# Second attention of a two-layer kernel: the output's division moves from VectorE to GpSimd, and its four turnings are spread over the loop

## What is computed

```
x = ln(x + block0(x))            # causal attention, 16 heads of 8, and more
x = ln(x + x @ w.T + pooled(x) @ disha)
qkv = x @ Wqkv + bqkv            # the second attention: no mask
scores = q @ k.T / sqrt(8)       # 16 heads, 1024 x 1024 per batch and head
attn = softmax(scores)
out = attn @ v                   # (sum of exp * v) / (sum of exp)
x = ln(x + out @ Wout + bout)
x = ln(x + relu(x @ W1 + b1) @ W2 + b2)
```

## Time and profile before

| | |
|---|---|
| median of 3 runs | 1514.3 us (1511.41 to 1517.33) |
| the profiled execution, its own time | 1513.78 us |
| its span in the trace | 1512.0 us |
| granted PE clock, mean over the span | 0.964 |
| PE busy over the span | 1366.1 us (90%) |
| DVE busy | 1251.6 us (83%) |
| ACT busy | 1079.6 us (71%) |
| POOL busy | 278.4 us (18%) |

### The profile page before, as it was taken

One profiled execution on the slowest core, in us unless ns is written; L12 is line 12 of the kernel. 1 busy time (PEld: TensorE's weight loads), 2 busy tenths in 40 slices (PEclk: granted clock), 3 DMA queues, 4 the chain that ended last, 5 costly groups with the idle time before them and its releaser, 6 DMA issues.

```text
span 1512.0 us, 31977 instructions
## 1 busy us (share of the span) xinstructions
PE 1366.1 (90%) x13016; PEld 565.2 (37%) x13016; DVE 1251.6 (83%) x1715; ACT 1079.6 (71%) x1239; POOL 278.4 (18%) x624
## 2 busy tenths in 40 slices
PE   6699999999998768888679999999999999999886
PEld 3334434444443235456323332332333333323455
DVE  8988888888884386985899999999999999997043
ACT  6167777777777567763358888888888888888652
POOL 5022313222222151431100000000000000001252
PEclk9689999999999989999889999999999999999998
DMA  5510111101000000021110000000000000000001
GB/s 179 169 44 24 39 31 31 40 24 46 24 4 2 1 1 0 1 81 67 42 64 24 23 24 23 24 21 14 16 23 24 23 23 24 3 3 3 1 15 42
DMA packets 38995, 47.90 MB, mean 32 GB/s; under 512 B 11072, under 2 KB 20160, under 8 KB 38720
## 3 DMA queue, kind: packets, MB, share of 16 engines
q1 hardware_dynamic: 38416, 45.31, 9.8%
q10 hardware_dynamic: 432, 0.53, 0.1%
HBM read 30.22 MB, written 15.47 MB: 30 GB/s over the span
## 4 chain that ended last, share of the span: by engine, by line
PE 73%; DVE 11%; ACT 7%; issue 5%; POOL 3%; DMA 1%; ACTq 0%; POOLq 0%; SPq 0%; DVEq 0%
PE ps L428 29%; PE ps L406 15%; PE ps L385 12%; PE ps L554 7%; DVE l_negp L326 3%; PE ps L445 3%; ACT l_outT L304 2%; ACT shared L298 2%; POOL n_rs L516 2%; PE ps L391 2%; DVE n_bst L497 1%; PE ps L547 1%; PE ps L1042 1%; PE ps L910 1%; PE ps L562 1%
## 5 line engine op out<-in xcount | busy, mean ns | idle before, releaser
L326 DVE TENSOR_REDUCE l_negp<-ps 128x2 f32<-128x1024 f32 (+2 forms) x832 | 956.4, 1181 | 57.7 <-PE ps L391 33.3
L298 ACT ACTIVATE shared<-ps 128x1024 f32<-128x1024 f32 (+1 forms) x832 | 820.5, 991 | 185.3 <-PE ps L406 155.7
L428 PE MATMUL ps<-shared,l_vs 128*32 128x256 f32 (+3 forms) x6648 | 515.4, 385 | 18.9 <-ACT l_outT L304 14.1
L385 PE MATMUL ps<-Ks,Qs 48*128 48x512 bf16 (+3 forms) x1792 | 329.2, 368 | 31.1 <-DVE l_negp L326 22.0
L406 PE MATMUL ps<-Qs,Ks 51*128 51x512 bf16 (+3 forms) x1792 | 321.1, 367 | 14.5 <-ACT shared L298 6.3
L428 PEld LDWEIGHTS ps<-shared,l_vs 128*32 128x32 f32 x6648 | 136.6, 108 | 198.0 <-issue 163.4
L406 PEld LDWEIGHTS ps<-Qs,Ks 51*128 51x128 bf16 x1792 | 81.1, 93 | 316.8 <-issue 181.3
L385 PEld LDWEIGHTS ps<-Ks,Qs 48*128 48x128 bf16 x1792 | 87.5, 94 | 171.8 <-ACT shared L298 96.0
L282 POOL TENSOR_SCALAR_AFFINE_SELECT shared<-shared 128x512 f32<-128x512 f32 x128 | 81.7, 640 | 311.1 <-ACT shared L298 309.0
L267 POOL CAST l_parts<-l_negm 128x16 bf16<-128x16 f32 x64 | 12.6, 197 | 442.3 <-DVE l_negm L331 439.2
L391 PE MATMUL ps<-mask,id 64*128 64x128 bf16 x1024 | 68.5, 222 | 0.0
(11 more groups left out here) (160 smaller groups left out, 1094.7 us busy)
## 6 DMA issues: line engine op xcount, KB each, us to landing
Qs<-scr_q SPq DMA_DIRECT2D x128, 64.0 KB
Ks<-scr_k SPq DMA_DIRECT2D x64, 96.0 KB
Qs<-scr_q SPq DMA_DIRECT2D x128, 32.0 KB
Ks<-scr_k SPq DMA_DIRECT2D x64, 64.0 KB
scr_q<-own SPq DMA_DIRECT2D x4, 768.0 KB, 3.6
scr_q<-shared SPq DMA_DIRECT2D x4, 768.0 KB, 3.5
scr_k<-own SPq DMA_DIRECT2D x4, 768.0 KB, 4.9
scr_k<-shared SPq DMA_DIRECT2D x4, 768.0 KB, 4.8
```

The costliest lines, as they stand in the source:

```text
L298: act.activation(dst, src, ACT.Exp, scale=SCALE).then_inc(exped, 1)
L326: dve.tensor_reduce(dst, src, AX_X, ALU.max, negate=True).then_inc(reduced, 1)
L385: last = pe.matmul(outs[par], Qs[s][r:r + MROW, h2, qt * P:(qt + 1) * P], Ks[s][r:r + MROW, h2, at:at + w], start=True, stop=True)
L428: last = pe.matmul(pv_ps[32 * h:32 * h + 32, a:a + wide], vs[g % 2][:, kt, h, :], pT[m % PRING][:, h, a:a + wide], start=m == u.first_step ...
```

## The change

For q = 32 to 61 the division leaves DVE. ACT copies what the turnings left in RING, 144 columns (4 query tiles x 4 heads x 8 values and their sum), to `sums` in SBUF, at tick E + 8; POOL raises the sums to the power -1 (a tensor of -1.0 as exponent) and multiplies into `attn_tm`. `sums` has two buffers; the copy waits for the division of two half groups back. RING is free for the next "turn_max" when ACT has copied. For q = 32 to 62 the four turnings stand at E + 4, E + 5, E + 7 and E + 8, each behind that tick's weigh step; q = 63 and the first attention keep all four at E + 4, and q = 62 and 63 keep the division on DVE. The pieces of the diff are, in this order, of `Units.order`, `gpsimd`, `scalar`, `vector`, `slot_free` and `tensor`.

```diff
+def turn_at(q):
+    return (4, 5, 7, 8) if NPER <= q < 2 * NPER - 1 else (4, 4, 4, 4)
+def off_vector(q):
+    return NPER <= q < 2 * NPER - QH
...
-                    (self.k_ends[q] + 2, ("evacuate", q)), (self.k_ends[q] + 4, ("turn_out", q))]
+                    (self.k_ends[q] + 2, ("evacuate", q)), (self.k_ends[q] + turn_at(q)[-1], ("turn_out", q))]
+            out += [(self.k_ends[q] + at, ("turn_part", q, t)) for t, at in enumerate(turn_at(q)[:-1])]
...
+        elif entry[0] == "turn_out" and off_vector(entry[1]):
+            q = entry[1]
...
+            pool.wait_ge(out_copied, q - NPER + 1)
+            pool.wait_ge(normed, q)
+            pool.tensor_tensor(rc[:, :, :], sums[q % 2][:, :, :, HD], minus_one[:, :, :], ALU.pow).then_inc(recips, 1)
+            pool.wait_ge(recips, q + 1)
...
+            pool.tensor_tensor(dst.rearrange("p t (h d) -> p t h d", d=HD), sums[q % 2][:, :, :, 0:HD],
+                               rc[:, :, :].unsqueeze(3).to_broadcast([P, CT, GH, HD]), ALU.mult).then_inc(normed, 1)
...
+        elif entry[0] == "turn_out" and off_vector(entry[1]):
+            q = entry[1]
+            act.wait_ge(out_turned, q + 1)
+            if q >= NPER + 2:
+                act.wait_ge(normed, q - 1)
...
+            act.activation(sums[q % 2][:, :, :, :], src[:, :, :, 0:HD + 1], ACT.Copy).then_inc(out_copied, 1)
...
-        elif entry[0] == "turn_out":
+        elif entry[0] == "turn_out" and not off_vector(entry[1]):
...
+        elif kind == "turn_out" and not off_vector(i):
+            pe.wait_ge(normed, i + 1)
         elif kind == "turn_out":
-            pe.wait_ge(normed, i + 1)
+            pe.wait_ge(out_copied, i - NPER + 1)
...
-            for t in range(CT):
-                last = pe.transpose(to[:, t * P:(t + 1) * P], outT[:, t * P:(t + 1) * P], ident)
-            last.then_inc(out_turned, 1)
+            last = pe.transpose(to[:, t * P:(t + 1) * P], outT[:, t * P:(t + 1) * P], ident)
+            if t == CT - 1:
+                last.then_inc(out_turned, 1)
```

More of the change, by code:

```diff
@@ L166, in order @@
             out += [(self.m_ends[q] - ahead, ("split", q)), (self.m_ends[q] - 1 - ahead + 4, ("turn_max", q)),
-                    (self.k_ends[q] + 2, ("evacuate", q)), (self.k_ends[q] + 4, ("turn_out", q))]
-        kinds = ("split", "key", "max", "weigh", "evacuate", "turn_max", "turn_out")
+                    (self.k_ends[q] + 2, ("evacuate", q)), (self.k_ends[q] + turn_at(q)[-1], ("turn_out", q))]
+            out += [(self.k_ends[q] + at, ("turn_part", q, t)) for t, at in enumerate(turn_at(q)[:-1])]
+        kinds = ("split", "key", "max", "weigh", "evacuate", "turn_max", "turn_part", "turn_out")
         return [(t - start, e) for t, e in sorted(out, key=lambda x: (x[0], kinds.index(x[1][0]), x[1][1:]))]
@@ L190, in attention @@
     rc = sb("rc", [P, CT, GH], F32)
+    sums = [sb(f"sums{i}", [P, CT, GH, HD + 1], F32) for i in range(2)]
+    minus_one = sb("minus_one", [P, CT, GH], F32)
     pv_ps = ps[:, 6 * BANK:7 * BANK]
@@ L199, in attention @@
     max_rows = [sem(f"max_rows{i}") for i in range(4)]
-    (scored, reduced, masked, evacuated, out_turned, recips, max_split, split_part,
+    (scored, reduced, masked, evacuated, out_turned, out_copied, recips, max_split, split_part,
      max_turned, max_copied, max_stored, v_clear, v_ready, cleared, joined) = (sem(n) for n in (
-         "scored reduced masked evacuated out_turned recips max_split split_part "
+         "scored reduced masked evacuated out_turned out_copied recips max_split split_part "
          "max_turned max_copied max_stored v_clear v_ready cleared joined").split())
@@ L244, in clear_values @@
             pool.memset(vs[i][:, :, :, HD:HD + 1], 1.0).then_inc(v_clear, 1)
-        pool.wait_ge(v_clear, 4)
+        pool.memset(minus_one[:, :, :], -1.0).then_inc(v_clear, 1)
+        pool.wait_ge(v_clear, 5)
     def values(pool, g):
@@ L273, in gpsimd @@
             pool.tensor_tensor(to[:, 2, :], rest[:, :], to[:, 1, :], ALU.subtract).then_inc(max_split, 1)
+        elif entry[0] == "turn_out" and off_vector(entry[1]):
+            q = entry[1]
+            at, qh = divmod(q - NPER, QH)
+            b, n = divmod(at, NG)
+            if n == 0 and qh == 0:
+                pool.wait_ge(handed.parted[1][0], b + 1)
+            pool.wait_ge(out_copied, q - NPER + 1)
+            pool.wait_ge(normed, q)
+            pool.tensor_tensor(rc[:, :, :], sums[q % 2][:, :, :, HD], minus_one[:, :, :], ALU.pow).then_inc(recips, 1)
+            pool.wait_ge(recips, q + 1)
+            dst = attn_tm[:, b * QT + qh * CT:b * QT + (qh + 1) * CT, n * GH * HD:(n + 1) * GH * HD]
+            pool.tensor_tensor(dst.rearrange("p t (h d) -> p t h d", d=HD), sums[q % 2][:, :, :, 0:HD],
+                               rc[:, :, :].unsqueeze(3).to_broadcast([P, CT, GH, HD]), ALU.mult).then_inc(normed, 1)
         elif entry[0] == "key":
@@ L311, in scalar @@
             act.activation(msp[q % 2][:, :], src, ACT.Copy).then_inc(max_copied, 1)
+        elif entry[0] == "turn_out" and off_vector(entry[1]):
[3 more added lines that the diff above has]
+                act.wait_ge(normed, q - 1)
+            src = slot(entry)[:, 0, :].rearrange("p (t h c) -> p t h c", t=CT, h=GH)
+            act.activation(sums[q % 2][:, :, :, :], src[:, :, :, 0:HD + 1], ACT.Copy).then_inc(out_copied, 1)
     def clear_maxima(dve):
@@ L438, in tensor @@
             pe.transpose(to, parts[q % 2].rearrange("p s c -> p (s c)"), ident_bf).then_inc(max_turned, 1)
-        elif entry[0] == "turn_out":
+        elif entry[0] in ("turn_part", "turn_out"):
             q = entry[1]
-            slot_free(pe, entry)
-            pe.wait_ge(evacuated, q + 1)
-            to = slot(entry)[:, 0, :]
-            for t in range(CT):
-                last = pe.transpose(to[:, t * P:(t + 1) * P], outT[:, t * P:(t + 1) * P], ident)
-            last.then_inc(out_turned, 1)
+            t = entry[2] if entry[0] == "turn_part" else CT - 1
+            if t == 0:
+                slot_free(pe, ("turn_out", q))
+                pe.wait_ge(evacuated, q + 1)
+            to = slot(("turn_out", q))[:, 0, :]
+            last = pe.transpose(to[:, t * P:(t + 1) * P], outT[:, t * P:(t + 1) * P], ident)
+            if t == CT - 1:
+                last.then_inc(out_turned, 1)
     def bank_free(pe, what):
@@ L1102, in __init__ @@
                     had[b] = (held.pop(b), b)
[L1103 to L1106, removed]
+            elif entry[0] in ("turn_max", "turn_part") and RING not in held:
+                if entry[0] == "turn_max" or entry[2] == 0:
+                    entry = entry if entry[0] == "turn_max" else ("turn_out", entry[1])
+                    self.slot[entry], self.before[entry] = RING, had[RING]
+                    had[RING] = entry
+            elif entry[0] in ("key", "max", "turn_max"):
                 at = next(s for s in ((at + n) % RING for n in range(1, RING + 1)) if s not in held)
```

## The result

The changed kernel takes 1523.22 us (median of 5 runs, 1519.67 to 1523.76), 1.0046 of the kernel before, 95 % interval [1.0026, 1.0066]. The forecast was 1521.0. By its bound of 0.5 % this counts as no change, though the interval lies wholly above 1. The ratio is the one on record; the two medians, 1523.22 and 1514.3, are 8.9 us (0.59 %) apart. The profiled execution took 1521.5 us with a span of 1519.6.

A forecast was written before the change was run, and what follows sets the result against it. A PE-ACT loop, not DVE, was taken to bound the kernel. 29 periods x (20.35 - 20.12) = +6.7 us, other parts 0, gave 1520.5 profiled and a median of 1521.0 us (+0.44%); range 1508 to 1531.

The forecast's parts named there:

- its bound of 0.5 %: Least difference, 7.6 us, that the prediction held a measurement of this kernel can tell from no change.
- The bound: Second attention: a PE-ACT loop of key product, exp, max product, weigh step sets the pace, 2.40 us per two ticks; not DVE.
- Rival E: DVE in the second attention is the bound after all; its 0.46 a period returns: 13.3 us faster, 1501; chance 0.05.
- The lone turning: PE, behind a weigh step: a turning alone costs 0.26 us; four are 1.04 in place of the block's 0.58.
- B: PE, turning to next key product: a lone turning costs its whole record, 0.33; +14.8 us, 1529; chance 0.17.
- C: PE: a lone turning costs the maxima's 0.17; period 20.00, -3.5 us, 1510.8; chance 0.12.
- D: PE: weights are loaded ahead, a lone turning costs 0.11; period 19.85, -7.8 us, 1506.5; chance 0.08.
- The period: Half group of the second attention, longest path through PE and ACT steps: 20.35 us against 20.12 before, over 29 periods.
- K(5) to K(10): PE key products of ticks 5 to 10, whose steps on the forecast path carry all four lone turnings at 0.26 each.
- The copy: ACT, 144 columns between the exps of E + 8 and E + 9: takes 0.3 us, cost taken 0.
- POOL: Power at most 4.5 us and product 0.46 per half group, behind the splitting of the maxima; nothing but the copy waits.
- DVE's division: Reciprocal 0.26 and product 0.29 on DVE while PE does the turnings; removing them alone is worth 0.

The follow-up runs named there:

- Short exps: Kernel before, with exp on only 256 of each 512 query columns in the second attention: 0.9743, 1474.9 us.
- short reductions: Kernel before, with each reduction over half its columns in the second attention: 0.9972, 1510.03 us.
- the spreading alone: Kernel before with only the turnings spread over ticks 4, 5, 7 and 8, division staying on DVE: 1.0044, 1521.65 us.
- the wide copy: Changed kernel with ACT copying all 512 columns of the turned output instead of the 144 used: 1.0072, 1524.55 us.
- the block with the division on GpSimd: Changed kernel with all four turnings together at E + 4 again, division still on GpSimd (POOL): 0.9995, 1514.08 us.

## Why the prediction was right, point by point

- **The bound** held. Short exps took 1.23 us from the period, short reductions nothing. Rival E, by which DVE's relief returns 13 us, is out: taking the division off DVE changed the period by 0.006 or less in each of four pairs of kernels.
- **The lone turning** was put at 0.26 from the load that the first of the block shows and the passage behind the fourth. It is 0.26 at all four places, so rivals B (0.33), C (0.17) and D (0.11) are out. A lone turning's weight load starts together with it (both 925.18), where in the block of the earlier trace rows the second load starts at 919.84 and its product at 919.95: the 0.06 is a load that nothing covers, as put. What the other 0.09 is, 0.20 to the key product in place of a step of 0.11, was not tried. The rule that D drew on, in the Trainium skill, "TensorE: Matmul & The Clock Gate" (Step-by-step: what each phase is for), that weight loads are pulled ahead of running products, shows here inside the block and not for a lone turning.
- **The period** was 20.35 by the path, 20.343 measured, with K(5) to K(10) on their places and no alternation; +6.7 us forecast, +6.6 measured. The remainder to the medians, 8.9 us apart, lies outside the loop or in the scatter of runs; the spreading alone, whose loop is the same, measured [1.003, 1.0059]. The scatter goes with the granted clock: of the runs of the kernel before, the fastest took 1509.87 at 0.968 and the slowest 1523.26 at 0.952. So the period was right by its mechanism, and that the whole came out at +0.46 % against +0.44 % is partly luck: the forecast put nothing outside the loop, and in the two profiles +4.0 and -3.1 largely cancel.
- **The copy** was put at 0.3 and free: 0.29, and free. What failed is the margin: I gave 0.3 of delay, 0.17 in hand and 0.13 of cost for a full 0.59; the wide copy shows 0.16, some 0.09 and 0.07. The path lacked the edge from K(1) over the exp to the evacuation. It does not bind in the changed kernel.
- **POOL** was put at 4.5 and 0.46 as upper bounds; the power took 2.90 and the product 0.41, hidden, as the block with the division on GpSimd confirms.
- **DVE's division** was worth 0, as put.

No kernel here that does the whole work beats the one before. By the prices found, a block of four behind a weigh step, at E + 4 or E + 10, is the cheapest place tried; other ticks were not run.

## What to carry to other kernels

Find the loop that sets the period and price the passages on it, not the instructions: four turnings of the same work cost 0.58 together and 1.04 apart, so on this loop small PE work belongs in one block. An engine that reads 97 % busy may still have room, when its records lap; here unloading it was worth nothing in the loop. Work given to an engine that executes in order must stand behind whatever the loop needs from it: the same 3.3 us on POOL cost nothing behind the split of the maxima and 0.6 us a period ahead of it.

## What was not expected of the hardware

- A turning of 128 x 128 costs more between a key and a max product than behind a weigh step (a pair 0.46 against 0.37): it starts 0.32 behind a key product where a max product starts 0.23 behind one. Why was not tried.
- The power on 16 columns takes 2.90 us where 4 columns take 1.12, which would be 0.15 us a column and 0.5 besides, if it goes straight between them.
- On ACT the next activation's record starts 0.11 before the end of the copy of 512 columns (928.41 and 928.30), so ACT takes its next instruction before the copy's record ends.
